# A graph attention kernel whose masks are kept in 128 rows and whose queries come in one transfer

## The reference

```
h = relu(layernorm(x));  x = x + relu(norm * segment_sum((norm * h @ W)[src], dst) + b)
for l in range(2):
    q, k, v = projections of x, 8 heads of 64
    scores  = (q[tgt] * k[srcidx]).sum(-1)            # one for each edge and head
    w       = segment_softmax(scores, tgt)
    x = batchnorm(x + segment_sum(w * v[srcidx], tgt) @ Wo.T + bo)
    x = batchnorm(x + relu(x @ W1.T + b1) @ W2.T + b2)
return x0 + layernorm(x)
```

## Time and profile before

| | |
|---|---|
| median of 3 runs | 3422.78 us (3419.57 to 3431.2) |
| the profiled execution: its time | 3425.16 us |
| its span, first to last instruction | 3423.3 us |
| busy: TensorE, VectorE, ScalarE, GpSimd | 3052.8, 2274.0, 1953.9, 2149.5 us |
| the 16 DMA engines, queue of SP and its transposes | 67.6% of the span |
| mean granted TensorE clock | 0.968 |

### The profile page before, as it was taken

One profiled execution on the slowest core, in us unless ns is written; L12 is line 12 of the kernel. 1 busy time (PEld: TensorE's weight loads), 2 busy tenths in 40 slices (PEclk: granted clock), 3 DMA queues, 4 the chain that ended last, 5 costly groups with the idle time before them and its releaser, 6 DMA issues. The chain is left out here.

```text
span 3423.3 us, 72330 instructions
## 1 busy us (share of the span) xinstructions
PE 3052.8 (89%) x24802; PEld 2399.2 (70%) x24802; DVE 2274.0 (66%) x6951; ACT 1953.9 (57%) x3918; POOL 2149.5 (63%) x1979
## 2 busy tenths in 40 slices
PE   2368999978869999999999989989999999999985
PEld 2124665545547888888888877767888888888874
DVE  8594433432337888888887853227888888888856
ACT  0124444433337777777777721227777778777724
POOL 1686778777527777777777710007777777777734
PEclk9999999989989999999999999999999999999987
DMA  9666666545589999999999921239999999989851
GB/s 371 98 129 158 124 118 131 113 93 98 90 201 175 166 170 166 170 163 172 163 168 160 156 75 29 52 70 181 169 165 167 166 172 168 169 165 175 151 119 60
DMA packets 1297462, 496.76 MB, mean 145 GB/s; under 512 B 1237240, under 2 KB 1262865, under 8 KB 1291408
## 3 DMA queue, kind: packets, MB, share of 16 engines
q1 hardware_dynamic: 1156197, 460.22, 67.6%
q0 software_dynamic: 133120, 0.80, 4.1%
q10 hardware_dynamic: 7788, 31.21, 2.7%
HBM read 153.55 MB, written 80.48 MB: 68 GB/s over the span
## 5 line engine op out<-in xcount | busy, mean ns | idle before, releaser
L1476 DVE CUSTOM_DVE_ANT_0 prob<-s_ps,mask 125x500 f32<-125x500 f32 x1600 | 1058.9, 673 | 277.8 <-PE s_ps L1323 201.8
L1253 POOL TENSOR_TENSOR staged<-prob,staged 125x500 f16<-125x500 f32 x960 | 1061.7, 1112 | 166.3 <-ACT staged L1247 103.8
L1413 ACT ACTIVATE prob<-prob,neg_max 125x1000 f32<-125x1000 f32 (+1 forms) x960 | 954.6, 994 | 117.5 <-DVE scrap L1482 114.7
L1323 PE MATMUL s_ps<-keys,queries 128*125 128x500 f16 x3200 | 944.5, 377 | 40.3 <-DMA queries<-q_tiles 27.4
L529 POOL DMA_INDIRECT counts<-count,cell x320 | 654.5, 2045 | 257.9 <-issue 96.4
L1354 PEld LDWEIGHTS o_ps<-values,across 125*125 125x125 f16 x7680 | 590.3, 138 | 196.8 <-issue 51.7
L1354 PE MATMUL o_ps<-values,across 125*125 125x128 f16 x7680 | 606.5, 222 | 33.8 <-DMA across<-staged 33.0
L1247 POOL CAST staged<-prob 125x500 f16<-125x500 f32 x640 | 385.5, 602 | 368.2 <-ACT prob L1413 238.5
L1489 DVE TENSOR_TENSOR p_lo<-t_ps,p_hi 125x500 f16<-125x500 f32 x640 | 432.1, 675 | 91.5 <-ACT p_hi L1423 91.1
L1334 PE MATMUL t_ps<-identity,prob 125*125 125x125 f32 x2560 | 411.8, 283 | 2.7 <-ACT agg L1433 2.5
L1423 ACT CAST p_hi<-t_ps 125x500 f16<-125x500 f32 x640 | 361.0, 564 | 85.1 <-PE t_ps L1334 84.5
(11 more groups left out here) (159 smaller groups left out, 3676.2 us busy)
## 6 DMA issues: line engine op xcount, KB each, us to landing
mask<-bias_rows SPq DMA_DIRECT2D x200, 218.8 KB
counts<-xt ACTq DMA_DIRECT2D x8, 3054.0 KB, 37.3
keys<-counts SPq DMA_DIRECT2D x40, 546.9 KB
bias_rows<-edge_bias SPq DMA_DIRECT2D x20, 1093.8 KB
queries<-q_tiles SPq DMA_DIRECT2D x80, 250.0 KB, 3.9
pair_row<-pair_flat SPq DMA_DIRECT2D x40, 437.5 KB
across<-staged SPq DMA_TRANSPOSE x960, 3.3
q_tiles<-q_both SPq DMA_DIRECT2D x80, 125.0 KB, 3.0
```

The costliest lines, as they stand in the source:

```text
L1253: engine.tensor_tensor(here[0:P, BPC:2 * BPC, 0:P], prob[u % PROBS][:, k * KC:(k + 1) * KC].rearrange("p (s c) -> p s c", s=BPC), here[0:P ...
L1323: mm = pe.matmul(s_ps[n % SB][:, 0:KC], lhsT=queries[b][:, h, part, :], rhs=keys[:, h, c * KC:(c + 1) * KC], start=(part == 0), stop=(part ...
L1413: act.activation(here, here, ACT.Exp, bias=neg_max[u % 4][:, :], accum_out=sums[u // H % 2][:, u % H, piece:piece + 1]).then_inc(exped, 1)
L1476: dve.tensor_tensor_reduce(out=prob[u % PROBS][:, at], in0=s_ps[n % SB][:, 0:KC], in1=bias[b][:, at], scale=1.0, scalar=MASKED, op0=ALU.ad ...
```

## The change

`bias_rows` becomes NT * 128 rows high, each mask tile in SBUF 128 rows high, and the mask moves 128 rows at a time with one DMA where there were two, in the store and in both layers' loads. Rows 125 to 127 are padding; VectorE clears rows 96 to 127 of the two front tiles once. The queries' two copies come in one DMA, whose source is the tile's 64 rows with an added outermost dimension of 2 and stride 0. The counts that are waited for follow.

```diff
-    bias_rows = dram("bias_rows", [N, N], F32)
+    bias_rows = dram("bias_rows", [NT * 128, N], F32)
...
-            bias = [sb(second, f"edge_bias{b}", [P, N]) for b in range(2)]
+            bias = [sb(second, f"edge_bias{b}", [128, N]) for b in range(2)]
...
-                    store_rows(sp, bias_rows[t * P:(t + 1) * P, :], bias[t % 2][:, :], bias_stored[t % 2])
+                    sp.dma_start(bias_rows[t * 128:(t + 1) * 128, :], bias[t % 2][:, :]).then_inc(bias_stored[t % 2], 16)
...
                 dve.wait_ge(bias0_loaded, 16)
+                for b in range(2):
+                    steps.done(dve.memset(bias[b][96:128, :], 0.0))
+                steps.wait()
...
-        bias = [sb(ctx, f"mask{b}", [P, N]) for b in range(2)]
+        bias = [sb(ctx, f"mask{b}", [128, N]) for b in range(2)]
...
                 def load_queries(t):
-                    for half in range(2):
-                        sp.dma_start(queries[t % 2][64 * half:64 * half + 64, :, :, :].rearrange("d h s n -> d (h s n)"),
-                                     q_tiles[t * DH:(t + 1) * DH, :]).then_inc(q_loaded[t % 2], 16)
+
+                    sp.dma_start(queries[t % 2][:, :, :, :].rearrange("p h s n -> p (h s n)"),
+                                 q_tiles[t * DH:(t + 1) * DH, :].unsqueeze(0).broadcast_to([2, DH, H * 2 * P])).then_inc(q_loaded[t % 2], 16)
 
                 def load_mask(t, c):
                     at = slice(c * KC, (c + 1) * KC)
-                    for p0, p1 in CUTS:
-                        sp.dma_start(bias[t % 2][p0:p1, at], bias_rows[P * t + p0:P * t + p1, at]).then_inc(mask_loaded[t % 2], 16)
+                    sp.dma_start(bias[t % 2][:, at], bias_rows[t * 128:(t + 1) * 128, at]).then_inc(mask_loaded[t % 2], 16)
...
-                        pe.wait_ge(q_loaded[b], 32 * ((T0 + u // H) // 2 + 1))
+                        pe.wait_ge(q_loaded[b], 16 * ((T0 + u // H) // 2 + 1))
...
-                            dve.wait_ge(mask_loaded[b], BOTH * NKC * ((T0 + u // H) // 2 + 1))
+                            dve.wait_ge(mask_loaded[b], 16 * NKC * ((T0 + u // H) // 2 + 1))
```

More of the change, by code:

```diff
@@ L494, in _ @@
                 for b in range(2):
-                    sp.wait_ge(bias_stored[b], BOTH * NT // 2)
+                    sp.wait_ge(bias_stored[b], 16 * NT // 2)
                 sp.wait_ge(qkv_stored[(NT - 1) % 2], QKV * (STAGED // 2) + 32)
@@ L691, in least @@
                     if t >= 2:
-                        dve.wait_ge(bias_stored[b], BOTH * (t // 2))
+                        dve.wait_ge(bias_stored[b], 16 * (t // 2))
                     for k in range(NKC):
-                        dve.tensor_scalar(bias[b][:, piece(k)], cnt[b][:, piece(k)], 1.0, None, ALU.max).then_inc(least_ready, 1)
+                        dve.tensor_scalar(bias[b][0:P, piece(k)], cnt[b][:, piece(k)], 1.0, None, ALU.max).then_inc(least_ready, 1)
                 def mask(t):
@@ L699, in mask @@
                     for k in range(NKC):
-                        dve.scalar_tensor_tensor(bias[b][:, piece(k)], cnt[b][:, piece(k)], MASKED, bias[b][:, piece(k)],
+                        dve.scalar_tensor_tensor(bias[b][0:P, piece(k)], cnt[b][:, piece(k)], MASKED, bias[b][0:P, piece(k)],
                                                  ALU.mult, ALU.add).then_inc(bias_ready, 1)
@@ L769, in logarithm @@
                     act.wait_ge(least_ready, NKC * (t + 1))
-                    act.activation(bias[t % 2][:, :], bias[t % 2][:, :], ACT.Ln).then_inc(log_ready, 1)
+                    act.activation(bias[t % 2][0:P, :], bias[t % 2][0:P, :], ACT.Ln).then_inc(log_ready, 1)
                 def absent(t):
@@ L1475, in add_bias @@
                     at = slice(c * KC, (c + 1) * KC)
-                    dve.tensor_tensor_reduce(out=prob[u % PROBS][:, at], in0=s_ps[n % SB][:, 0:KC], in1=bias[b][:, at],
+                    dve.tensor_tensor_reduce(out=prob[u % PROBS][:, at], in0=s_ps[n % SB][:, 0:KC], in1=bias[b][0:P, at],
                                              scale=1.0, scalar=MASKED, op0=ALU.add, op1=ALU.max,
```

## The result

The changed kernel takes 3756.73 us (median of 4 runs, 3753.43 to 3765.06) against 3421.18 us for the kernel before (4 runs). The ratio is 1.0978, 95% interval 1.096 to 1.0995: 9.8% slower. Forecast were 3810 us, 11%, and a range of 3620 to 4080. The profiled execution has a span of 3751.3 us, 328 us over the one of before.

A forecast was written before the change was run, and what follows sets the result against it. Attention was taken as bound by TensorE, its transposes having little slack. Stop 8.0 plus clock 2.7 less recovery 0.4 gave 10.3 us a tile, 371 for 36 tiles; with 16 for starts, about 3810 us, range 3620 to 4080.

The forecast's parts named there:

- Two engines at 24.4 GB/s: Attention's query load: outermost dimension 2 puts it on 2 DMA engines, 10.5 us a tile where it took 2.3.
- Rival B: Query load spreads over 16 engines after all: 3420 us, chance 0.12, or 3392 to 3408 us, chance 0.04.
- Rival C: Query load: a lone engine reaches only 15 GB/s, 16.8 us lost a tile, 4060 us; chance 0.12.
- D: Query load on 2 engines but softer stops without a clock fall, 6 us a tile, 3650 us; chance 0.12.
- The stop: Attention: the first transpose behind each query load has no slack, so TensorE stops 8.0 us a tile.
- The clock: Attention, after each stop: TensorE runs 5.5 us at half clock and loses 2.7 us a tile.
- Recovery: Attention: other engines fill buffers during the stop, so 0.4 of TensorE's usual 0.8 us idle a tile goes.
- The starts: Start of each attention layer, tiles 0 and 1: about 8 us lost a layer, 16 in all.
- The masks: Attention's mask loads, one transfer for two: 200 SP instructions fewer, 80 us of SP's work, no gain taken.
- The front stage: Mask stores before attention: one of two SP instructions saved, 8 us at most, taken as 0.
- The clearing of the padding rows: Front stage: VectorE's clearing of both masks takes 6.8 us, hidden in 9.1 us of idle before the first merge.

The follow-up runs named there:

- e3: Changed kernel with queries in four transfers without broadcast, each copy's 64 rows cut into 62 and 2: 3762.12 us, ratio 1.1028.
- e4: Changed kernel with queries in four transfers without broadcast, each copy's 64 rows cut into 51 and 13: 3574.06 us, ratio 1.0471.
- e6: Changed kernel with queries stored twice in DRAM, a tile loaded by one 128-row DMA without broadcast: 3395.24 us, ratio 0.9935.
- e5: Changed kernel with its one-transfer query load issued from ScalarE's queue instead of SyncE's: 3735.07 us, ratio 1.0936.
- e1: Changed kernel with queries loaded as before, in two transfers of 64 rows (masks change alone): 3400.92 us, ratio 0.9969.
- e9: Changed kernel with each broadcast query load cut by columns into 4 pieces, one ahead of each of the first four units: 3637.75 us, ratio 1.0629.

## Why the prediction was right, step by step

**Two engines at 24.4 GB/s.** Right, from the one row that bore on it: the changed kernel shows 1.9 engines and 48 GB/s, the packets of the load shown start between 1171.65 and 1182.35, 10.7 us for the forecast 10.5, and e3, e4 and e6 confirm the rule for 62, 51 and 128 rows. Rival B is out. Rival C is too: an engine that works alone reached 24 GB/s, not the 15 of the busy stretches. So is D: the clock did fall, and the loss a tile is 8.8 us, not 6.

**The stop.** Forecast 8.0 us a tile. The 36 long waits for transposes (7.2 to 9.3 us) have a mean of 7.9. In the timeline shown it is 8.58 us, and TensorE's start at L1357 moved from 6.3 to 14.6 us after the load's issue, 8.3 later. The waits in sum rose by 297.9 - 33.0 = 265 us, or 7.4 us for each of 36 loads; this sum has the recovered idle time already in it. The size was right. The mechanism was right only in part: I had the transposes waiting because they stand behind the load in one queue, with 14 of their 16 shares going on. e5 shows that another queue helps little (ratio 1.0936 for the changed kernel's 1.0978), and the slices from 1174 and 1178 that the transpose's other packets stand too. The size came out all the same, since by either mechanism the first transpose ends when the load does; that part was luck.

**The clock.** Forecast 2.7 us a tile; this term was mis-sized. TensorE's busy time rose by 3117.1 - 3052.8 = 64.3 us, 1.8 a tile. The fall of the clock is there with all 36 stops, but it lasts 4.8 us behind a stop on average (2.8 to 6.1; 4.5 in the stop shown) where I took 5.5, which makes 2.4 of the 2.7. What brings the 2.4 down to 1.8 isn't shown; I suppose that TensorE isn't limited by its clock at every moment of that time.

**Recovery.** Forecast 0.4 us of 0.8; from the totals, 7.4 + 1.8 = 9.2 us of stop and clock a tile. The span gives 328 + 7 (front) - 19 (starts, next) = 316 us, 8.8 a tile. The rest, 0.4 us, is idle time elsewhere in TensorE that went: its waits for VectorE's `chunk_max` alone fell from 12.7 to 3.0 us. So this term was right. Forecast 10.3 a tile, measured 8.8.

**The starts.** Forecast 8 us a layer. TensorE's waits for queries, one a layer, are 46.2 us where they were 27.4, so 19 us for 16; in layer 0 it is 29.21 for the 20.01 of the earlier trace rows. The way was in part another: tile 1's queries went out at 988.72 instead of 997.45 and were out of the way when the first transpose was issued at 1008.98, which landed at 1012.5 and not near 1020.

**The masks.** I took nothing for them; they gain 11.6 us where nothing else stands in the way (e1). The row that told of the part in attention was there: 15.8 us of waits for transposes in the earlier trace rows, and SyncE issues them. In the changed kernel this gain isn't seen: 1.0978 with the masks, 1.0988 without, the intervals overlap, and they would allow e1's 12 us as well as none. The front stage I put at 0 with bounds of 0 and -8, because SyncE waits there for VectorE; its end came 7.4 us sooner in the changed kernel's trace and 12.9 in e1's, and no run shows why. The clearing of the padding rows showed no cost, as forecast: the two passes take 2.14 us each, the idle time before the first merge shrinks from 9.1 to 3.5 us, and the merge starts at 278.6 where it started at 279.6.

In all: 371 forecast for the tiles became 316, 16 became 19, 0 became -7, and 3812 became 3753 for the profiled execution (its span is 3751). Rival B counted 38 query issues saved; the earlier trace rows has 80, so it is 40, which changes none of its prices.

## What to carry to other kernels

Before two transfers are made one, look at the outermost dimension of both sides: the number of DMA engines was the largest number up to 16 that divides it (5 for 125 rows, 3 for 51, 2 for 62 and for a doubled source), and it can be read in a trace as the queue's share of the 16 engines while a transfer runs alone. A background transfer on few engines isn't harmless because nobody waits for it: find the transfer right behind it that has no slack. Where a source must be read twice, keeping it twice in DRAM was worth more than the saved bytes (0.9935 against 1.0978).

## What the hardware showed that was not expected

In these runs a transpose by DMA advanced on all of its engines only as fast as on the slowest. With two engines taken, 17 of its packets stood for 8.5 us or more in the changed kernel and no further one started until the load was through, and beside a load on another queue it moved 5.75 packets a microsecond on each (e5). SyncE also stands in the issue of such a transpose, up to 9.9 us where 1.2 is usual.

TensorE's granted clock fell with stops well short of the 7.21 and 8.10 us of the earlier trace rows: with 34 of the 37 of 2.3 to 5.0 us in e4, and with the one of 2.71 us in e9. A stop of e4 and what follows it (stretches, the clock third from last):

```profile
1161.90:1166.25 4.35, 0.00 (x1) 0.03 (x1) 1.28 (x3) 1.00 (x4) 0.00 (x0) 0.87 0.66 115
1166.25:1171.90 5.65, 5.65 (x34) 4.70 (x35) 3.44 (x10) 2.05 (x4) 4.90 (x6) 0.50 0.91 174
1171.90:1176.00 4.10, 4.10 (x47) 3.57 (x46) 3.20 (x11) 3.27 (x8) 2.94 (x4) 0.99 0.90 194
```

An idle time of 4.35 us is followed by 5.65 us at 0.50, as long as behind the one of 7.21 us in the earlier trace rows; over all such stops the low clock lasts 4.4 us behind a stop in e4 and 4.8 in the changed kernel. TensorE is busy 61 us more than in e1 in the first and 73 in the second. So shortening the stops from 8 to 3.5 us saved their length, but most of what the clock costs behind them stayed. The mean clock of that profiled execution is 0.949, against 0.971 for e1.
